# Graph layer with relation products on one core: VectorE makes the low halves of the first two products one unit behind, and the edge ordering starts three units ahead

## The reference

```python
h = maximum(layernorm(x), 0)                       # [1250, 1024]
out = h @ root + bias
for r in range(8):
    mask = (edge_type == r)
    sums = segment_sum(h[src] * mask[:, None], dst)   # over the edges
    cnt  = segment_sum(mask, dst)
    out += (sums / maximum(cnt, 1)) @ weight[r]
u = out
z = concat([u, h], axis=1) @ w_gate + b_gate
x + tanh(u) * z + h * (1 - z)
```

## Time and profile before

| | us |
|---|---|
| median of 3 runs | 1476.33 |
| lowest and highest run | 1475.23, 1481.91 |
| the profiled execution | 1475.66 |
| its span, first to last instruction | 1473.8 |
| TensorE busy in it | 1294.7 |
| VectorE busy | 938.9 |
| GpSimd busy | 728.8 |
| ScalarE busy | 409.2 |

### The profile page before, as it was taken

How to read it: one execution, slowest core, us unless ns; L and a number is a source line. 1 busy time by engine, 2 the same in 40 slices (tenths; PEclk the granted TensorE clock), 3 DMA queues, 4 the chain that set the end, 5 groups by cost and what they waited for, 6 DMA issues and landing times.

```text
span 1473.8 us, 19899 instructions
## 1 busy us (share of the span) xinstructions
PE 1294.7 (88%) x6165; PEld 650.2 (44%) x6165; DVE 938.9 (64%) x1256; ACT 409.2 (28%) x501; POOL 728.8 (49%) x801
## 2 busy tenths in 40 slices
PE   3998999999998299899898999998977878878996
PEld 1444444444443144444444454444433434444663
DVE  6587688575664366565465667666534556686766
ACT  5443223122333022321132143243202213343000
POOL 2422078787878556565645547444555454420000
PEclk9998999999999599999999999999999999999998
DMA  5542143252244266867664866774776855856676
GB/s 210 196 158 83 40 132 87 53 164 59 57 117 132 76 204 220 265 193 233 200 194 145 271 216 182 255 233 153 227 233 207 253 169 172 272 182 190 177 223 200
DMA packets 108104, 259.15 MB, mean 176 GB/s; under 512 B 20826, under 2 KB 21329, under 8 KB 108020
## 3 DMA queue, kind: packets, MB, share of 16 engines
q1 hardware_dynamic: 75204, 175.63, 36.2%
q0 software_dynamic: 32816, 82.39, 19.9%
HBM read 194.34 MB, written 82.17 MB: 188 GB/s over the span
## 4 chain that ended last, share of the span: by engine, by line
PE 33%; POOL 19%; DMA 19%; DVE 13%; issue 11%; ACT 3%; SPq 2%; POOLq 1%; DVEq 0%; ACTq 0%
PE ps L1285 25%; POOL table_rows L585 16%; DMA early<-y_rows,pair 13%; PE ps L1243 6%; DMA out_dram<-hT 3%; DVE W L914 2%; SPq L418 1%; POOL onehot L618 1%; DMA hT<-zh_rows 1%; DVE early L1113 1%; DVE hT L962 1%; ACT early L703 1%; POOL pair L600 1%; DVE yhl L1036 1%; DVE urow L1120 1%
## 5 line engine op out<-in xcount | busy, mean ns | idle before, releaser
L1285 PE MATMUL ps<-W,hT 128*128 128x512 f16 (+2 forms) x4860 | 1102.3, 385 | 9.3 <-DVE W L914 7.0
L1285 PEld LDWEIGHTS ps<-W,hT 128*128 128x128 f16 (+2 forms) x4860 | 494.1, 104 | 553.7 <-issue 46.2
L610 POOL DMA_INDIRECT early<-y_rows,pair x192 | 231.2, 1204 | 149.4 <-PE ps L1246 101.6
L1243 PE MATMUL ps<-early,onehot 128*125 x768 | 205.9, 398 | 107.6 <-POOL onehot L618 81.4
L585 POOL DMA_INDIRECT table_rows<-edges,table_i x160 | 241.7, 1511 | 114.1 <-issue 57.2
L618 POOL TENSOR_SCALAR onehot<-iota_d,pair 128x125 f16<-128x125 f16 x184 | 153.6, 835 | 201.1 <-DMA early<-y_rows,pair 197.8
L743 ACT ACTIVATE yhl<-W 128x512 f16<-128x512 f32 x120 | 75.3, 628 | 396.5 <-DVE W L1036 207.4
L1243 PEld LDWEIGHTS ps<-early,onehot 128*125 x768 | 104.8, 141 | 178.9 <-issue 128.8
L914 DVE SCALAR_TENSOR_TENSOR W<-W,wsc 128x2048 f16<-128x2048 f32 x65 | 152.5, 2351 | 24.0 <-ACT W L693 24.0
L693 ACT ACTIVATE W<-W,wsc 128x2048 f16<-128x2048 f32 x65 | 128.3, 1990 | 74.2 <-DVE W L930 35.9
L660 ACT ACTIVATE peek_out<-W 128x1024 bf16<-128x1024 f32 x84 | 88.4, 1052 | 98.3 <-DMA W<-in_L_gnn_weight_dram 73.4
(11 more groups left out here) (161 smaller groups left out, 676.1 us busy)
## 6 DMA issues: line engine op xcount, KB each, us to landing
y_rows<-yhl SPq DMA_DIRECT2D x144, 256.0 KB, 2.2
W<-in_L_gnn_weight_dram SPq DMA_DIRECT2D x32, 1024.0 KB, 6.9
early<-u_rows SPq DMA_DIRECT2D x40, 448.0 KB
u_rows<-early SPq DMA_DIRECT2D x40, 448.0 KB
W<-in_L_gnn_w_gate_dram SPq DMA_DIRECT2D x8, 1024.0 KB, 7.9
early<-in_x_dram SPq DMA_DIRECT2D x9, 512.0 KB, 4.4
hs_rows<-early SPq DMA_DIRECT2D x9, 512.0 KB, 2.9
u_rows<-yhl SPq DMA_DIRECT2D x18, 256.0 KB, 2.0
```

What stands on the lines that cost most here:

```text
L610: pool.indirect_dma_start(out=G[:, b, :], out_offset=None, in_=y_rows[i], in_offset=bass.IndirectOffsetOnAxis(ap=idx[:, b, :], axis=0), bo ...
L1243: nc.tensor.matmul(ps[0:DT, 4 + half, :], hot_t, rows[:, bass.ds(ring_slot * (2 * D) + (half * D + part * HC), HC)], start=first and part ...
L1285: last = nc.tensor.matmul(ps[0:rows, n % 4, :], hT[:, m, v_h, k, n0:n0 + rows], Wh[:, MAT[w][c], v_w, k, :], start=(first and v_h + v_w == ...
```

## The change

VectorE's `finish(n)` for units of rel0 and rel1 no longer makes the low half of unit n: it notes the unit, and the next step's `finish` makes it (`finish_plain`, called at the head of every `finish`). So at step n VectorE waits for ScalarE's copy of unit n-1. The scans stand at steps 4, 7, 10 and 12 in place of 5, 9, 13 and 15; the totals after unit 14 (17), the bounds after unit 16 (19), and the positions at steps 18, 22, 26 and 30 (21, 25, 29 and 33). Nothing else is edited.

```diff
-    KEYS_AT, SCAN_AT, TOTALS_AT, BOUNDS_AT = 2, {5: 0, 9: 1, 13: 2, 15: 3}, 17, 19
-    POSITIONS_AT = {21: 0, 25: 1, 29: 2, 33: 3}
+    KEYS_AT, SCAN_AT, TOTALS_AT, BOUNDS_AT = 2, {4: 0, 7: 1, 10: 2, 12: 3}, 14, 16
+    POSITIONS_AT = {18: 0, 22: 1, 26: 2, 30: 3}
...
+            plain = []
+
+            def finish_plain():
+
+                while plain:
+                    m = plain.pop()
+                    o = out_no(m)
+                    rows = LT[out_place(o)[1]][1]
+                    dve.wait_ge(s["y_hi"], HI_NO[o] + 1)
+                    nc.vector.scalar_tensor_tensor(out=yhl[0:rows, o % 4, 1, :], in0=ps[0:rows, m % 4, :], scalar=2.0 ** -Y_BITS,
+                                                   in1=yhl[0:rows, o % 4, 0, :], op0=ALU.mult,
+                                                   op1=ALU.subtract).then_inc(s[YDONE], 1)
+
             def finish(n):
                 w = w_of(n)
+                finish_plain()
                 p, i = divmod(n - FIRST[w], HT)
...
                 if w < PLAIN:
-                    rows = LT[out_place(o)[1]][1]
-                    dve.wait_ge(s["y_hi"], HI_NO[o] + 1)
-                    nc.vector.scalar_tensor_tensor(out=yhl[0:rows, o % 4, 1, :], in0=part[0:rows], scalar=2.0 ** -Y_BITS,
-                                                   in1=yhl[0:rows, o % 4, 0, :], op0=ALU.mult,
-                                                   op1=ALU.subtract).then_inc(s[YDONE], 1)
+                    plain.append(n)
                     return
```

## The result

The change is faster: the ratio of its time to that of before is 0.9928, 95% interval 0.9905 to 0.9951 (19 runs each; medians 1467.95 and 1478.48 us). By the ratio that is 10.7 us of the 1478.5, where 17.7 were forecast, and 1467.95 lies 0.95 us above the range of 1450 to 1467. The profiled execution took 1467.95 us with a span of 1466.2.

A forecast was written before the change was run, and what follows sets the result against it. TensorE's 31.8 us hole before the first edge sum, waiting for a table delayed by scatters behind `positions(0)`, was the largest loss; it closes by 25.7 - 8.0 = 17.7, so 1475.66 - 17.7 gives 1458 us, range 1450 to 1467.

The forecast's parts named there:

- L: How much later TensorE ends unit 20 than before, not regained up to the first edge sum; taken as 8.0 us.
- the walk: Hand-followed schedule of every engine over the first 20 units; unit 20 ends at 174.3 us, against 166.3 in the old order.
- the prediction's own sum: Shrinking of TensorE's hole before the first edge sum when VectorE's step 95 is last: 25.7 - 8.0 = 17.7 us.
- The hole and what bounds it: TensorE's 31.8 us idle before the first edge sum; ended by the scatters or VectorE's step 95, whichever is later.
- X: How much earlier `positions(0)` ends on VectorE, moving scatters and table with it; taken as 20.9 us.
- The keys ... end at 54.4: VectorE's edge keys at step 2 begin near 44.6 us, take 9.78 us and end at 54.4.
- I take 0: Extra time for edge keys meeting a GpSimd subtraction and another memset: possibly 0 to 4.9 us, taken as 0.
- Tile 5 ... just in time: Tile 5's low half, behind scan 0, ends at 78.7 us; TensorE reaches mid unit 7 at 78.1, no gap to speak of.
- The scans, 10.30 us each: Four VectorE scans (compare and count), the same work in another order, each taking 10.30 us as before.
- The gaps at tile 7, the totals and unit 20: New TensorE gaps at mid unit 10, after unit 14 and before unit 20: 5.8, 3.7 and 6.7 us.
- From the first sum to the end: Everything behind the first edge sum moves as a block, its time unchanged within 3 us.
- Case 3: Rival: more TensorE gaps, L of 12 to 18 us, time 1462 to 1468 us; chance 0.13.

The follow-up runs named there:

- lag_only: The change's one-unit lag of the low halves alone, with scans, totals, bounds and positions at the steps of before; ratio to before 0.9904, median 1464.15 us.
- weights_first: The change, with the first two quarters of rel1's weight halved on VectorE ahead of the first positions; ratio to before 0.991, median 1466.36 us.
- late_memsets: The change, with GpSimd's second to fourth pairs of scan-factor memsets one low half later; ratio to before 0.9914, median 1465.96 us.
- moves_only: The kernel before with the change's new step numbers, each low half still made in its own step; ratio to before 1.0026, median 1481.78 us.
- no_overlap: The change, with VectorE waiting for GpSimd's low half ahead of scans 1, 2 and 3; one run, 1473.32 us.
- no_read: The change, with GpSimd's subtraction for the low half of h replaced by a memset to zero; one run, 1460.38 us, beside 1471.08 of before.
- spread: The change, with scans 1 and 2, bounds and positions at earlier steps and rel1's weight quarters moved beside them; ratio to before 0.9889, median 1462.14 us.
- scan0_at5: The change, with scan 0 back at step 5, behind the statistics of tile 5; one run, 1471.60 us.

## Why the prediction was wrong

**The step that failed is "L: the walk gives 174.3 - 166.3 = 8.0. ... I take 8.0".** The mechanism held and the term was too small: L was 14.5 at unit 20 and 14.9 at unit 98. Put into the prediction's own sum, 25.7 - 14.9 = 10.8, where the first sum came 10.87 us earlier and the runs gained 10.7. That the runs meet it so closely is in part luck: the profiled execution gained 7.7, and the stretch behind the first sum varies by 7 us between executions. Three signs that the prediction had named failed with L: unit 20 ended beyond 180, `positions(0)` began at 160.4 and not at 152 to 156, and the scatters at 175.1 and not at 166 to 170.

Point by point:
- **The hole and what bounds it.** Right. In eight of the ten kernels VectorE's step 95 is last, and the first sum starts at 480.9 + L within 0.2 us, from L = 2.6 to L = 29.6. In lag_only and weights_first the scatters are last, and VectorE waits for the table.
- **X, taken as 20.9.** Also too hopeful: the scatters began 14.8 us earlier and ended 12.4 earlier. The units are late by what L is. It did not decide, but by 1 to 2 us only: the table was back at about 481.3 (its read was issued at 478.7 and landed 2.6 us later) and VectorE ready at 482.6. With the L that I took, 8.0, the scatters would have been the bound, as weights_first shows.
- **"The keys ... end at 54.4", and under unknown costs "I take 0".** Wrong. They ended at 58.26 after 12.94 us instead of 9.78. I had named the meeting with a subtraction and a memset, priced it at up to 4.9, and then let the walk say that "L stays within 0.5". late_memsets takes 2.8 us of it away, and unit 20 begins 3.15 us earlier. (At unit 98, which the first sum follows, 0.4 of it was left; the clock behind the gaps took the rest.) The walk had mistaken where VectorE becomes the late one: from scan 0 to the totals, 76 us, it stands idle for 9.
- **"Tile 5 ... just in time".** Wrong by the same 3 us, with scan 0 at 65.6 instead of 61.7: a gap of 4.72, and a restart.
- **The scans, 10.30 us each.** Three of four took 12.1. In the order of before each scan stood behind a wait for ScalarE's copy of the same unit, and GpSimd's subtraction was over by then, or within 0.2 us of it. The lag takes that wait away, and three of the moved scans share their step with a tile's statistics, so each comes right behind them and meets the subtraction that they release. moves_only has the same steps without the lag, and no long count. I weighed the exclusion of the two engines for the scatters, where it cost little more than before (300.1 us from the first to the last, 297.7 before), and not for the scans. no_overlap and no_read show that the 1.8 us are the overlap.
- Together some 3.2 + 5.4 us more on VectorE. With these waits put in, the same walk gives 13.4 for unit 20 instead of 8.0, near the 14.5 measured; its steps are not shown here. By experiment only the keys' part is priced apart. What the three long counts cost TensorE is not: no_read, which takes them away together with other work, has L = 2.7 at unit 20, well below the 8.0 of the walk, which had none of these waits. How much of that is the shorter work on GpSimd, and how much are other errors of the walk, is open.
- **The gaps at tile 7, the totals and unit 20.** 4.9, 5.5 and 7.1 against 5.8, 3.7 and 6.7: right in place, and near in size.
- **From the first sum to the end.** 970.5 us against 967.2, just outside the 3 us that I allowed. Over all eleven profiled executions this rest lies between 967.2 and 974.7 and does not follow the first sum, so I read no effect of the change in it. What makes it vary stays open.
- **The rivals.** Case 3, more gaps with L of 12 to 18, is what happened; it had 0.13, and "the walk has tile 5 on the edge" was its reason. Its own L of 14.9 gives 1464.9 from the profiled execution, inside the range; the 19 runs of before had their median 2.8 us above that execution, and this put the result just outside.
- **What the two parts are worth.** I forecast the sum and never the parts. The lag alone brings the gain (0.9904), the moved steps alone none (1.0026), and together they are not to be told from the lag (0.9928): the moved steps start the scatters 0.7 us earlier than lag_only and raise L by 22 us.

## What to carry to other kernels

When a wait is taken away, look at what that wait kept apart: here it held VectorE's long two-input work clear of GpSimd's subtraction, and the overlap cost 1.8 us each time on the engine that had just become the late one. A hand-followed schedule must carry such exclusions between engines, and must be tried with one duration 3 us longer before its sum is used. When two chains end within a few us of each other, take both bounds down together (spread did, weights_first did not): shortening one gains nothing, however large the gap that is removed.

## What the runs showed of the hardware that I had not expected

- Each side can be the one that waits, within one meeting: the subtraction of 89.85 waited 2.0 us for the compare, and the count behind the compare then waited 1.8 us for the subtraction. A memset on GpSimd, which reads nothing, held up a cast (L862, 4.90 us with it, 2.10 without) but in no_read all four compares (L961), 3.48 us each, met a memset and took no longer.
- A gap of 2.0 to 2.6 us on TensorE ahead of unit 89 cost nothing more in four executions (the 120 matmuls behind it took 26.06 us in before, the change, weights_first and no_read) and 1.3 to 1.7 us in the other seven (27.34 to 27.75). The granted clock tells them apart: over these 120 matmuls it was 1.00 in the four and 0.94 or 0.95 in the seven, where it was 0.50 to 0.71 in the 3 us behind the gap (0.50 is the lower of its two levels, 1.2 GHz). The gaps do not: the clock stayed at 1.00 behind 2.62 us in the change and fell behind 2.12 in spread. What decides is open.
- Behind the gap of 7.07 us at unit 20, of the same length in five kernels, the granted clock over 6 us was 0.78 (the change), 0.75 (no_read), 0.68 (scan0_at5, no_overlap) and 0.52 (late_memsets), and the next 360 matmuls took 79.14, 79.31, 79.74, 79.75 and 80.70 us. A gain of 2 to 3 us ahead of such a gap can be lost to the clock behind it.
